# A graph network kernel on one Trainium2 core: the next tile's exponential and first coarse level on ScalarE, ahead of a tile's last exact level

## The chip, the cores and the metric

The kernel runs on one core of one Trainium2 chip. The metric is the device time of one execution in microseconds (us), lower is better. Engines are called by their names and, in rows of the profile, by short forms: TensorE (PE, its weight loads PEld), VectorE (DVE), ScalarE (ACT), GpSimd (POOL) and SyncE (SP), which here issues the transfers.

## The reference

Two residual blocks on x (3327 x 256, float32). The second holds the work that the change touches: two diffusion steps, and in each an attention matrix whose rows are cut to their nucleus, the fewest largest probabilities that hold 90% of the mass.

```python
h = relu(layernorm(x)); x = x + L0_gnn(h, adj)          # A @ (h W + b) / deg
X = relu(layernorm(x))
S = adj + I; Rf = S / rowsum(S); Rb = S / colsum(S)
Xf = Xb = Xa = X; Z = 0
for s in range(2):
    logits = (Xa @ W1) @ W2 @ (Xa @ W3).T                # 3327 x 3327
    keep   = smallest set of largest softmax(logits) with mass >= 0.9, row by row
    A      = softmax(where(keep, logits, -inf))
    Xf, Xb, Xa = Rf @ Xf, Rb @ Xb, A @ Xa
    Z = Z + Xf @ U1[s] + Xb @ U2[s] + Xa @ U3[s]
x = x + layernorm(X + Z) * gamma + beta
```

## The kernel before

The 3327 rows are padded to 26 tiles of 128. Each diffusion step (`diffusion_step(0)`, then `diffusion_step(1)`; the change touches the second alone, "step one" in the code's counting, where `first` is false) runs one software pipeline over the tiles. Each engine has its own program, written out in order by hand: `step_sweep` calls the engine's `body(i)` for i from -2 to 27, and the engines meet only through semaphores. In `body(i)` four tiles are in hand: k = i-1 (its masked probabilities are multiplied with `xa`), i (VectorE searches its exact cut), j = i+1 (ScalarE and GpSimd narrow its threshold on whole rows) and m = i+2 (its logits, exponential and coarse levels).

The threshold of a tile is narrowed in six levels in step one. At each level ScalarE makes two passes over the probabilities (`sums(j, n)`, level e = n // 2): a Relu pass (line L895) and a Sign pass (L900), each with a sum over the row. Levels 0 to 2 are coarse and read 832 columns, levels 3 to 5 are exact and read all 3327. After the Sign pass GpSimd's `level(j, e)` works out the next threshold in four or five instructions on one column (L808 first), and the next level's Relu pass waits for it. So the passes are called here by their n: 0 to 5 coarse, 6 to 11 exact, even ones Relu and odd ones Sign. The level after pass 11 computes no threshold; it releases `p_ready`, for which VectorE's `search` of that tile waits.

ScalarE's program in `body(i)` of step one is, in this order: copy chunk 0 of the transposed tile k out of PSUM (L919, called C0 here), C1, the copy of z (L927), pass 6 of j, C2, pass 7 of j, C3, passes 8 and 9 of j, `xo` of k (L937), pass 10 of j, two copies into `zt` for k (L945, L948), pass 11 of j, the exponential of m (L877), passes 0 and 1 of m, two scaled copies out of the product of i, passes 2 and 3 of m, two more such copies, passes 4 and 5 of m. The table `STEPS` places passes 6 to 11 among the chunks.

GpSimd's program: the two additions of `spread(k)` (L781) and one of `add_z` (L787), the addition of the identity to the tile `at` (L838), levels 3, 4, 5 of j, then levels 0, 1, 2 of m.

VectorE's search of tile i, as far as it matters: a bracket of small operations from L1031, two whole-row passes (L1055, L1064), sixteen MAX8 (L1069), then the logits of tile m are taken out of PSUM in four chunks (`take_logits`, L1200), the row maximum of m is put down (`negmax`, L1205; the exponential of m waits for it), a ranking of the candidates, and last the mask, a whole-row subtraction (L1131), after which the next tile's search begins at once.

TensorE in `body(i)`: transposes of chunks 0 and 1 of k (L1338), product of chunk 0 (L1346), transposes 2, product 1, transposes 3, logits of m chunk 0 (L1311), product 2, logits 1, product 3, logits 2 and 3, some small transposes, the 52 products of tile i with the features (L1392), and the small products of z (L1400). Product 0 needs C0, logits 0 needs C2 (it reuses that bank), logits 1 needs C3. TensorE's `logits` of chunk 2 wait for VectorE to have taken chunk 0.

Of the kernel before, what the change touches and what calls it, by code (L numbers as in the profile page):

```python
# [44 lines left out]
def gnn_program(nc, x, adj, W, b, W1, W2, W3, U1, U2, U3, gamma, beta, out):  # L45
# [7 lines left out]
    T = -(-N // P)  # L53
# [19 lines left out]
    ACT_BISECTIONS = (3, 3)  # L73
# [599 lines left out]
    def diffusion_step(s):  # L673
# [29 lines left out]
        with nc.Block() as block:  # L703
# [66 lines left out]
            @block.gpsimd  # L770
            def _(pool):
                if first:
                    for v in pb:
                        nc.gpsimd.memset(v[:, N:NP], 0.0).then_inc(S("p_pad"), 1)

                def spread(i):

                    pool.wait_ge(S2("sx_lo")[i.slot], sums_copied(i))
                    after(pool, "fbT_psum", i + -1)
                    for n, dst in enumerate((xf_sb, xb_sb)):  # L780
                        nc.gpsimd.tensor_tensor(dst[i.slot][:, :], t_hi[:, n, :], t256[i.slot][:, n, :], ALU.add).then_inc(S2("xfb")[i.slot], 1)  # L781

                def add_z(k):

                    pool.wait_ge(S("z_copy"), k.t + 1)
                    pool.wait_ge(S2("y_loaded")[k.slot], 16 * (k.use_here + 1))
                    nc.gpsimd.tensor_tensor(y_sb[k.slot][:, :], z_sb, y_sb[k.slot][:, :], ALU.add).then_inc(S("y_sum"), 1)  # L787

                def goal(j):

                    u = j.third
                    pool.wait_ge(S("exp"), j.n + 1)
                    share = nucleus_pad[:, :] if j.t == T - 1 else NUCLEUS
                    nc.gpsimd.tensor_scalar(targets[u][:, :], mass[u][:, 0:1], share, None, ALU.mult)
                    ch.link(nc.gpsimd.tensor_scalar(over[u][:, 5:6], mass[u][:, 0:1], (NUCLEUS - 1.0) * WSUB / N, None, ALU.mult))

                def level(j, e):

                    if not j.inside(T) or e >= LEVELS[s][j.t]:
                        return  # L800
                    u, last, f = j.third, e == LEVELS[s][j.t] - 1, e - SUB
                    if e == 0:
                        goal(j)
                    o, g = over[u], f + 1
                    t = rough_t[u][:, e:e + 1] if f < 0 else thr[u][:, 2 + f:3 + f]
                    up, down = math.exp(MOVES[s][e]), math.exp(-MOVES[s][e])
                    pool.wait_ge(S3("sums")[u], levels_before(s, j.t) + e + 1)
                    ch.link(nc.gpsimd.tensor_scalar(o[:, 2:3], o[:, 1:2], float(WSUB if f < 0 else N), t, ALU.add, ALU.mult))  # L808
                    if f < 0:
                        m, enough = o[:, 3:4], o[:, 5:6]  # L810
                        ch.link(nc.gpsimd.tensor_scalar(m, o[:, 2:3], -0.5, o[:, 0:1], ALU.mult, ALU.add))  # L811
                    else:
                        m, enough = mass[u][:, 2 + f:3 + f], targets[u][:, :]
                        ch.link(nc.gpsimd.tensor_scalar(m, o[:, 2:3], 0.5, o[:, 0:1], ALU.mult, ALU.add))  # L814
                    if g < BISECTIONS[s]:
                        ch.link(nc.gpsimd.tensor_scalar(o[:, 4:5], m, enough, up - down, ALU.is_ge, ALU.mult))  # L816
                        if g < 0:
                            ch.link(nc.gpsimd.tensor_scalar(rough_t[u][:, e + 1:e + 2], o[:, 4:5], down, t, ALU.add, ALU.mult))  # L818
                        else:
                            ch.link(nc.gpsimd.tensor_scalar(thr[u][:, 2 + g:3 + g], o[:, 4:5], down, t, ALU.add, ALU.mult))  # L820
                            if not last:
                                ch.link(nc.gpsimd.tensor_scalar(minus_t[u][:, g:g + 1], thr[u][:, 2 + g:3 + g], -1.0, None, ALU.mult))  # L822
                    pool.sem_inc(S3("point")[u], 1)  # L823
                    if last:
                        pool.sem_inc(S("p_ready"), 1)  # L825

                pool.wait_ge(S("search_consts"), 1)
                ch = Chain(pool, f"step_levels_{s}")

                def body(i):  # L830
                    j, k, m = i + 1, i + -1, i + 2
                    if not first and k.inside(T):
                        spread(k)
                    if not first and (i + -2).inside(T):
                        add_z(i + -2)
                    if i.inside(T):
                        pool.wait_ge(S2("at_loaded")[i.slot], 16 * (i.use + 1))
                        nc.gpsimd.tensor_tensor(at[i.slot][:, i.t, :], at[i.slot][:, i.t, :], ident16[:, :], ALU.add)\  # L838
                            .then_inc(S2("st_ready")[i.slot], 1)
                    for e in range(EARLY, SUB + ACT_BISECTIONS[s]):  # L840
                        level(j, e)
                    if not first:
                        level(m, 0)
                    if first and k.inside(T):
                        pool.wait_ge(S2("xfb")[k.slot], 2 * (k.use + 1))
                        pool.wait_ge(S2("fb_stored")[1 - k.slot], 16 * (k + 1).use)
                        ch.add(nc.gpsimd.tensor_copy(fb_sb[:, 0:D], xf_sb[k.slot][:, :]))
                        ch.link(nc.gpsimd.tensor_scalar(xk_sb[:, :], xb_sb[k.slot][:, :], kappa[:, :], None, ALU.mult))
                        ch.link(nc.gpsimd.tensor_copy(fb_sb[:, 2 * D:3 * D], xk_sb[:, :]))
                        nc.gpsimd.tensor_tensor(fb_sb[:, D:2 * D], xf_sb[k.slot][:, :], fb_sb[:, 0:D], ALU.subtract)\  # L850
                            .then_inc(S2("fb_lo")[k.slot], 1)
                        nc.gpsimd.tensor_tensor(fb_sb[:, 3 * D:4 * D], xk_sb[:, :], fb_sb[:, 2 * D:3 * D], ALU.subtract)\
                            .then_inc(S2("fb_lo")[k.slot], 1)
                    if not first:
                        level(m, 1)
                        level(m, 2)
                step_sweep(pool, body)
                if not first:
                    pool.wait_ge(sem("scale_in"), 32)
                    pool.wait_ge(sem("x1_in"), 16)  # L860
                    for t in range(T):
                        nc.gpsimd.tensor_tensor(x1_in[:, t, :], x1_in[:, t, :], beta_bc, ALU.add).then_inc(sem("x1_beta"), 1)

            @block.scalar
            def _(act):
                act.wait_ge(S("search_consts"), 1)

                STEPS = ((), (0,), (1,), (2, 3), (4,), (5,)) if first else ((), (6,), (7,), (8, 9), (10,), (11,))
                relus = Chain(act, "step_relu_sum", base=sum(sum(LEVELS[q]) for q in range(s)))
                signs = {}  # L870

# [32 lines left out]
                def body(i):  # L904
# [34 lines left out]
                    if j.inside(T):  # L939
                        for n in STEPS[NT]:  # L940
                            sums(j, n)
                    if k.inside(T):
                        act.wait_ge(S("fbT_psum"), k.n + 1)
                        act.wait_ge(S("z_psum"), k.n)
                        nc.scalar.activation(zt[:, 0:4, :].rearrange("p k c -> p (k c)"), bank[7][:, :], ACT.Copy,  # L945
                                             scale=(1.0 / SCALE if first else 1.0)).then_inc(S("fbT"), 1)
                        act.wait_ge(S("xoT_psum"), k.n + 1)
                        nc.scalar.activation(zt[:, 4:6, :].rearrange("p k c -> p (k c)"), bank[4][:, D:2 * D], ACT.Copy).then_inc(S("xoT"), 1)  # L948
# [1 line left out]
                        for n in STEPS[NT + 1]:  # L950
                            sums(j, n)
                    if m.inside(T):
                        exponentials(m)
                    if not first and m.inside(T):
                        for n in range(0, 2):
                            sums(m, n)
                    if i.inside(T):
                        act.wait_ge(S("sx_psum"), i.n + 1)
                        if first:
# [3 lines left out]
                        else:  # L963
                            act.wait_ge(S2("xfb")[1 - i.slot], 2 * (i + 1).use)
                            for n, sc in enumerate((rinv_s, cinv_r)):
# [2 lines left out]
                                nc.scalar.activation(t256[i.slot][:, n, :], bank[5 + n][:, D:2 * D], ACT.Copy, scale=sc[:, i.t, :])\  # L968
                                    .then_inc(S2("sx_lo")[i.slot], 1)
                                if n == 0 and m.inside(T):  # L970
                                    for q in range(2, 4):
                                        sums(m, q)
                    elif not first and m.inside(T):
                        for q in range(2, 4):
                            sums(m, q)
                    if not first and m.inside(T):
                        for n in range(4, 6):
                            sums(m, n)
                    if not first and i.static and i.t == T - 1:
                        layernorm_sqrt(act, 2, 0, T - 2)  # L980
                step_sweep(act, body)
# [452 lines left out]
```

## Time and profile before

| what | us |
|---|---|
| median of 3 runs | 2497.32 |
| lowest, highest | 2494.7, 2497.5 |
| the profiled execution | 2493.01 |
| its span, first to last instruction | 2491.2 |
| its mean granted TensorE clock | 0.921 of full speed |

The page of the profile gives each engine's busy time as a share of the span. The trace below it has every instruction's start and length; a number in square brackets behind an instruction is the time its engine was idle just before it, and who ended that idle time. A start of an instruction can lie a little before the end of the one ahead of it, since instructions of one engine overlap by about 0.1 us, so distances are read from start to start.

### The profile page before, as it was taken

What the parts mean: (1) busy time and instruction counts of PE and PEld (TensorE: products, weight loads), DVE (VectorE), ACT (ScalarE), POOL (GpSimd) and SP (SyncE); (2) the same over time, 40 slices, a digit from 0 to 9 for tenths busy, and PEclk for the clock granted to TensorE, in tenths of its full rate; (3) what the DMA queues carried; (4) which work ended last, traced back from release to release, by engine and by line L of the source; (5) the groups of instructions that cost most, each with busy time, mean ns of one, the idle gap of its engine ahead of it and who ended that gap; (6) DMA issues with size and microseconds to landing.
All of it is one profiled execution on the core that took longest, in us unless ns stands there. A gap on an engine that the chain in (4) does not pass through costs nothing.

```text
span 2491.2 us, 33017 instructions
## 1 busy us (share of the span) xinstructions
PE 1956.3 (79%) x10002; PEld 1286.8 (52%) x10002; DVE 1924.2 (77%) x6082; ACT 1700.4 (68%) x1806; POOL 838.4 (34%) x1438
## 2 busy tenths in 40 slices
PE   2999565999999999998548778778778678688693
PEld 1555333666666666666325455445455455455462
DVE  6777658888888888887386887877877878878876
ACT  4434147888888888886367777777777677677640
POOL 2000043444444444444243343333332332333423
PEclk9999887999999999999869989989989989889896
DMA  6777220111111111111510100001001001001013
GB/s 228 286 284 278 103 65 18 49 48 49 49 48 49 48 48 48 48 48 39 180 61 1 39 20 25 34 20 38 20 20 39 20 20 39 20 20 39 19 47 140
DMA packets 65726, 167.62 MB, mean 67 GB/s; under 512 B 7037, under 2 KB 45307, under 8 KB 61947
## 3 DMA queue, kind: packets, MB, share of 16 engines
q1 hardware_dynamic: 65530, 165.43, 19.1%
q8 instruction: 72, 1.18, 0.2%
q14 instruction: 124, 1.02, 0.1%
HBM read 117.95 MB, written 47.45 MB: 66 GB/s over the span
## 4 chain that ended last, share of the span: by engine, by line
ACT 21%; issue 13%; POOL 13%; PE 4%; DVE 1%; POOLq 0%; DMA 0%; ACTq 0%; DVEq 0%; SPq 0%
ACT junk_a L900 10%; ACT junk_a L895 8%; POOL over L808 7%; PE banks L1346 3%; POOL over L816 1%; ACT pt L919 1%; POOL over L811 1%; POOL rough_t L818 1%; POOL points L820 1%; DVE region L1274 1%; POOL minus_t L822 1%; POOL points L814 1%; DVE region L1269 0%; ACT zt L945 0%; PE banks L1338 0%
## 5 line engine op out<-in xcount | busy, mean ns | idle before, releaser
L1346 PE MATMUL banks<-xa,pt 128*128 128x256 f32 x2704 | 683.2, 407 | 232.7 <-ACT pt L919 232.7
L1346 PEld LDWEIGHTS banks<-xa,pt 128*128 128x128 f32 x2704 | 534.0, 204 | 389.1 <-ACT pt L919 245.1
L895 ACT ACTIVATE junk_a<-pb_all,minus_t 128x3327 f16<-128x3327 f32 x151 | 463.9, 3072 | 221.2 <-POOLq L823 220.9
L900 ACT ACTIVATE junk_a<-pb_all,minus_t 128x3327 f16<-128x3327 f32 x151 | 463.0, 3066 | 1.8
L1392 PE MATMUL banks<-region,at 128*128 128x512 f16 x2028 | 448.9, 381 | 0.0
L808 POOL TENSOR_SCALAR over<-over,points 128x1 f32<-128x1 f32 x151 | 104.5, 692 | 881.3 <-ACT junk_a L900 881.2
L1200 DVE TENSOR_SCALAR_CACHE_REDUCE pb_all<-banks 128x1024 f32<-128x1024 f32 x260 | 210.9, 848 | 225.9 <-PE banks L1311 223.7
L1392 PEld LDWEIGHTS banks<-region,at 128*128 128x128 f16 x2028 | 199.1, 98 | 230.1 <-issue 4.1
L1311 PE MATMUL banks<-keys,qs 64*128 64x512 f32 (+1 forms) x832 | 199.9, 577 | 88.4 <-DVE pb_all L1200 49.2
L808 POOL TENSOR_SCALAR over<-over,rough_t 128x1 f32<-128x1 f32 x78 | 185.1, 2373 | 169.2 <-ACT junk_a L900 169.1
L1338 PE MATMUL banks<-ident,pb_all 128*128 128x128 f32 x1352 | 181.6, 281 | 54.5 <-DVE pb_all L1131 34.4
L1069 DVE MAX8 junk_v<-below 128x8 f32<-128x208 f32 (+1 forms) x624 | 222.4, 432 | 2.2
L919 ACT ACTIVATE pt<-banks 128x896 f32<-128x896 f32 x208 | 172.6, 857 | 51.2 <-PE banks L1338 51.1
L895 ACT ACTIVATE junk_a<-pb_all,rough_t 128x832 f16<-128x832 f32 x78 | 77.1, 988 | 180.5 <-POOLq L823 179.6
L1338 PEld LDWEIGHTS banks<-ident,pb_all 128*128 128x128 f32 x1352 | 159.1, 145 | 68.0 <-issue 56.5
L1064 DVE SCALAR_TENSOR_TENSOR below<-pb_all,cur 128x3327 f32<-128x3327 f32 x52 | 191.6, 3684 | 1.9
L877 ACT ACTIVATE pb_all<-pb_all,negmax 128x3327 f32<-128x3327 f32 x52 | 159.3, 3063 | 12.9 <-DVE negmax L1205 12.9
L1311 PEld LDWEIGHTS banks<-keys,qs 64*128 64x128 f32 x832 | 69.4, 193 | 173.7 <-DVE pb_all L1200 70.1
L1017 DVE SCALAR_TENSOR_TENSOR below<-pb_all,points 128x3327 f32<-128x3327 f32 x31 | 114.2, 3685 | 51.7 <-POOLq L825 51.5
L533 PE MATMUL banks<-region,at 128*128 128x512 f16 x676 | 151.8, 382 | 0.0
L1400 PE MATMUL banks<-u_sb,zt 128*128 128x256 f32 x624 | 148.5, 388 | 1.1 <-ACT zt L948 1.1
L1128 DVE MATCH_REPLACE8 below<-junk_v,below 128x208 f32<-128x208 f32 x416 | 143.5, 359 | 0.0
(222 smaller groups left out, 2859.7 us busy)
## 6 DMA issues: line engine op xcount, KB each, us to landing
at<-adjT_d SPq DMA_DIRECT2D x52, 832.0 KB, 4.8
region<-in_adj_dram SPq DMA_DIRECT2D x25, 1663.5 KB, 8.0
adjT_d<-at SPq DMA_DIRECT2D x26, 832.0 KB, 3.9
fb_d<-fb_sb SPq DMA_DIRECT2D x26, 256.0 KB, 2.0
region<-fb_d SPq DMA_DIRECT2D x2, 3328.0 KB, 19.0
y_d<-y_sb SPq DMA_DIRECT2D x50, 128.0 KB, 1.9
x_d<-pb_all SPq DMA_DIRECT2D x1, 3328.0 KB, 10.4
qs<-q_d SPq DMA_DIRECT2D x104, 32.0 KB, 4.1
```

The costliest lines, as they stand in the source:

```text
L808: ch.link(nc.gpsimd.tensor_scalar(o[:, 2:3], o[:, 1:2], float(WSUB if f < 0 else N), t, ALU.add, ALU.mult))
L877: nc.scalar.activation(p, p, ACT.Exp, bias=negmax[u][:, :], accum_out=mass[u][:, 0:1]).then_inc(S("exp"), 1)
L895: nc.scalar.activation(junk_a[:, 0:w], pb[u][:, 0:w], ACT.Relu, scale=sign, bias=t, accum_out=over[u][:, 0:1])\
L900: nc.scalar.activation(junk_a[:, 0:w], pb[u][:, 0:w], ACT.Sign, scale=sign, bias=t, accum_out=over[u][:, 1:2])\
L919: nc.scalar.activation(pt[sl][:, 0:n * P], pt_ps[sl][:, 0:n * P], ACT.Copy).then_inc(S2("pt")[sl], 1)
L1064: ch.link(nc.vector.scalar_tensor_tensor(out=below[:, 0:N], in0=p, scalar=cut, in1=p, op0=ALU.is_lt, op1=ALU.mult, accum_out=below_sum[:, :]))
L1069: ch.add(nc.vector.max(cand[:, 8 * g:8 * g + 8], below[:, g * W8:(g + 1) * W8]))
L1200: nc.vector.tensor_scalar(halves_of_p[:, h:h + n, a:a + w], halves_of_bank[:, h:h + n, 0:w], 1.0, -3.0e38, ALU.mult, ALU.max, accum_out=mi ...
L1311: nc.tensor.matmul(pt_ps[c % 2][:, h * CW:h * CW + w], qs[j.slot][r, :], keys[r, s * HW + c0:s * HW + c0 + w], start=True, stop=True).then ...
L1338: last = nc.tensor.transpose(pt_ps[sl][:, t * P:(t + 1) * P], p[:, (t0 + t) * P:(t0 + t + 1) * P], ident[:, :])
L1346: last = nc.tensor.matmul(bank[4][:, 0:D], pt[sl][:, t * P:(t + 1) * P], xa[:, t0 + t, :], start=(t0 + t == 0), stop=(t0 + t == T - 1))
L1392: last = nc.tensor.matmul(bank[5 + n][:, :], at[i.slot][:, t, :], mov, start=(t == 0), stop=(t == T - 1))
```

## The change

In step one the passes of a body are put in another order. ScalarE runs passes 6 and 7 of j together after C1 (before: 6 before C2, 7 after it). The exponential of m and its passes 0 and 1 move from behind pass 11 to ahead of pass 10, right after `xo`. Passes 2 and 3 of m follow pass 11 directly, passes 4 and 5 of m stand between the two pairs of scaled copies. GpSimd takes level 0 of m ahead of level 5 of j. No instruction is added or removed; step zero is as it was.

```diff
-                    for e in range(EARLY, SUB + ACT_BISECTIONS[s]):
+                    for e in range(EARLY, SUB + ACT_BISECTIONS[s] - 1):
                         level(j, e)
                     if not first:
                         level(m, 0)
+                    level(j, SUB + ACT_BISECTIONS[s] - 1)
...
-                STEPS = ((), (0,), (1,), (2, 3), (4,), (5,)) if first else ((), (6,), (7,), (8, 9), (10,), (11,))
+                STEPS = ((), (0,), (1,), (2, 3), (4,), (5,)) if first else ((), (6, 7), (), (8, 9), (), (11,))
...
+                    if not first:
+                        if m.inside(T):
+                            exponentials(m)
+                            for n in range(0, 2):
+                                sums(m, n)
+                        if j.inside(T):
+                            sums(j, 10)
                     if k.inside(T):
                         act.wait_ge(S("fbT_psum"), k.n + 1)
                         act.wait_ge(S("z_psum"), k.n)
...
                     if m.inside(T):
-                        exponentials(m)
-                    if not first and m.inside(T):
-                        for n in range(0, 2):
-                            sums(m, n)
+                        if first:
+                            exponentials(m)
+                        else:
+                            for n in range(2, 4):
+                                sums(m, n)
...
                                 if n == 0 and m.inside(T):
-                                    for q in range(2, 4):
+                                    for q in range(4, 6):
                                         sums(m, q)
                     elif not first and m.inside(T):
-                        for q in range(2, 4):
+                        for q in range(4, 6):
                             sums(m, q)
-                    if not first and m.inside(T):
-                        for n in range(4, 6):
-                            sums(m, n)
```

## Rows read from the trace of the kernel before

**Rows 1.** The page, busy time of each engine over the span.

```profile
PE 1956.3 (79%) x10002; PEld 1286.8 (52%) x10002; DVE 1924.2 (77%) x6082; ACT 1700.4 (68%) x1806; POOL 838.4 (34%) x1438
```

**Rows 2.** Who waited for whom, 1330.6 to 2344.7 us: total, times, longest.

```profile
ACT junk_a L895 <- POOLq L823: 249.4, 110, 4.1
DVE pb_all L1200 <- PE banks L1311: 192.6, 66, 5.7
```

**Rows 3.** Timeline of ScalarE: C0 of body 1 and of body 24.

```profile
1301.68 1.70 ACT L919 ACTIVATE pt<-banks 128x896 f32<-128x896 f32 x2
...
2362.75 0.89 ACT L919 ACTIVATE pt<-banks 128x896 f32<-128x896 f32 x1
```

**Rows 4.** Timeline of ScalarE, one body, from pass 2 to pass 0.

```profile
1801.89 0.99 ACT L895 ACTIVATE junk_a<-pb_all,rough_t 128x832 f16<-128x832 f32 x1 [4.06 <-POOLq L823]
...
1803.01 0.99 ACT L900 ACTIVATE junk_a<-pb_all,rough_t 128x832 f16<-128x832 f32 x1
...
1807.69 0.99 ACT L895 ACTIVATE junk_a<-pb_all,rough_t 128x832 f16<-128x832 f32 x1 [2.88 <-POOLq L823]
...
1809.79 1.70 ACT L919 ACTIVATE pt<-banks 128x896 f32<-128x896 f32 x2
...
1813.48 3.07 ACT L895 ACTIVATE junk_a<-pb_all,minus_t 128x3327 f16<-128x3327 f32 x1 [1.71 <-POOLq L823]
...
1816.54 0.90 ACT L919 ACTIVATE pt<-banks 128x896 f32<-128x896 f32 x1
1817.34 3.06 ACT L900 ACTIVATE junk_a<-pb_all,minus_t 128x3327 f16<-128x3327 f32 x1
...
1822.36 3.07 ACT L895 ACTIVATE junk_a<-pb_all,minus_t 128x3327 f16<-128x3327 f32 x1 [1.28 <-POOLq L823]
...
1825.56 3.07 ACT L900 ACTIVATE junk_a<-pb_all,minus_t 128x3327 f16<-128x3327 f32 x1
...
1830.59 3.07 ACT L895 ACTIVATE junk_a<-pb_all,minus_t 128x3327 f16<-128x3327 f32 x1 [1.51 <-POOLq L823]
...
1834.39 3.07 ACT L900 ACTIVATE junk_a<-pb_all,minus_t 128x3327 f16<-128x3327 f32 x1
...
1837.45 3.06 ACT L877 ACTIVATE pb_all<-pb_all,negmax 128x3327 f32<-128x3327 f32 x1
...
1840.63 0.99 ACT L895 ACTIVATE junk_a<-pb_all,rough_t 128x832 f16<-128x832 f32 x1
```

**Rows 5.** Timeline of TensorE, the same body: product 0, logits 0.

```profile
1810.74 4.79 PE L1346 MATMUL banks<-xa,pt 128*128 128x256 f32 x14 [8.42 <-ACT pt L919]
...
1819.80 1.13 PE L1311 MATMUL banks<-keys,qs 64*128 64x512 f32 x4
```

**Rows 6.** Timeline of VectorE, the same body.

```profile
1796.88 3.62 DVE L1131 TENSOR_TENSOR pb_all<-pb_all,below 128x3327 f32<-128x3327 f32 x1
...
1802.68 3.69 DVE L1055 SCALAR_TENSOR_TENSOR below<-pb_all,cur 128x3327 f32<-128x3327 f32 x1
...
1808.16 3.68 DVE L1064 SCALAR_TENSOR_TENSOR below<-pb_all,cur 128x3327 f32<-128x3327 f32 x1
...
1821.09 1.23 DVE L1200 TENSOR_SCALAR_CACHE_REDUCE pb_all<-banks 128x1024 f32<-128x1024 f32 x1 [4.37 <-PE banks L1311]
...
1830.48 0.16 DVE L1205 TENSOR_REDUCE negmax<-junk_v 128x1 f32<-128x5 f32 x1
...
1842.41 3.62 DVE L1131 TENSOR_TENSOR pb_all<-pb_all,below 128x3327 f32<-128x3327 f32 x1
```

**Rows 7.** Timeline of GpSimd: L808 behind a coarse and behind an exact pass.

```profile
1804.19 2.31 POOL L808 TENSOR_SCALAR over<-over,rough_t 128x1 f32<-128x1 f32 x1 [2.37 <-ACT junk_a L900]
...
1820.59 0.26 POOL L808 TENSOR_SCALAR over<-over,points 128x1 f32<-128x1 f32 x1 [4.45 <-ACT junk_a L900]
```

**Rows 8.** Timeline of VectorE in body 0: the one search that waits for its levels.

```profile
1286.87 0.23 DVE L1031 TENSOR_SCALAR least<-points,target 128x5 f32<-128x5 f32 x1 [0.66 <-POOLq L825]
```

**Rows 9.** Busy time by stretch: us, engines, granted clock (PEclk), DMA. One product 0.

```profile
1856.30:1862.00 5.70, 5.70 (x14) 4.53 (x15) 5.62 (x20) 3.99 (x4) 4.71 (x9) 0.53 0.00 0
```

## The prediction

> **What bounds the kernel now.** I read the busy times first: TensorE, VectorE and ScalarE are at 79, 77 and 68% [rows 1], so no engine is the bound by itself and the time lies in how they wait for each other. Next the period of a body: C0 of body 1 to C0 of body 24 is 1061.07 us, 23 bodies, 46.13 us each [rows 3]. Then the waits between engines [rows 2]: ScalarE waited 249 us for GpSimd, VectorE 193 us for logits. The timeline of one body tells which of the two is cause. ScalarE stands before five passes for GpSimd's next threshold: 4.06 (pass 2), 2.88 (4), 1.71 (6), 1.28 (8), 1.51 us (10), together 11.4 us, a quarter of the period; it waits for nothing else of size [rows 4]. TensorE meanwhile stands 8.4 us until C0 lets it do product 0 [rows 5], and the logits behind it reach VectorE 4.4 us late [rows 6]. ScalarE and GpSimd handing one tile's threshold to and fro, with nothing of another tile in between, is the loop that sets the end. VectorE's own work is 46.1 less 193/22 = 8.8 us, some 37.4 us a body: the floor if ScalarE's waits went.
>
> **The prices.** All start to start.
> - ScalarE [rows 4]: coarse Relu to Sign 1.12, Sign to next 0.99, exact Relu to Sign 3.20 (3.06 with a copy between), Sign to next 3.06, exponential to pass 0 3.18, a chunk copy 0.80 (0.60 for the last), zt copies 0.74 (pass 10 to 11 is 3.80), a scaled pair 0.7 (pass 4 would be free at 1807.69-2.88 = 1804.81, 0.8 behind pass 3's 0.99).
> - An exact level: Sign 1817.34, L808 3.25 later, next Relu 1.77 after that [rows 4, 7]: 5.02 from Sign to Relu.
> - A coarse level: Sign 1803.01, L808 1.18 later, but it lasts 2.31 instead of 0.26 us, to 1806.50; VectorE's L1055 ends at 1806.37 [rows 6, 7]. GpSimd stands still until such a whole-row operation ends, plus 0.13 us. The same holds for L1131 and L1064. From the end of L808 to the next Relu is 1.19 us; undisturbed, 1.18 + 0.26 + 1.19 = 2.63 from Sign to Relu. The level that leads from coarse to exact takes 0.3 more (1.50).
> - VectorE [rows 6], from L1131: L1055 at +5.80, L1064 at +11.28. Logits 0 on TensorE to the row maximum is 1830.64-1819.80 = 10.84 us [rows 5, 6], from there to the next L1131 11.77 us. C0 to product 0 is 0.95, product 0 to logits 0 9.06.
>
> A rule bears on the port. The Trainium skill, SBUF — State Buffer, section "SBUF: two separate sides", says that the port pair of VectorE and GpSimd is locked for the whole instruction by whoever starts first, and the other stands still. The 2.31 us and the 0.13 us behind L1055's end agree. By the same rule GpSimd could also hold VectorE off, which no row here shows: `spread`'s addition would come just as L1064 wants to start. That would make L1064 late by one addition, and logits 0 with it; as VectorE then still has room before logits 1, the sum is the same by the rule and without it.
>
> **The change, walked through.** Nothing is added: the work is the same and only the waits move. I count from the exponential E, which now stands ahead of pass 10 and needs the row maximum N of m; say E = N+0.1.
> - Pass 0 at E+3.18, pass 1 4.30, pass 10 5.4 (its level was asked for at pass 9; no wait), zt copies 8.5, pass 11 9.2, pass 2 12.4, pass 3 13.5, scaled pair 14.5. Pass 2's threshold is asked for at 5.5 and ready long before; the wait of 4.06 is gone. The zt copies end 9.7 behind N; TensorE needs them only after its 52 products, about N+10: hidden, with half a us to spare.
> - Level 5 of j: L808 at 9.2+3.25 = 12.5. L1131 starts at N+11.77, E+11.7, ends 15.3. L808 is held until 15.4, and `p_ready` comes near 15.9. VectorE, free at 15.2, waits 0.7 us. Body 0 shows this very case, 0.66 us [rows 8].
> - Level 1 of m is queued behind it: L808 at 16.0, pass 4 at 17.5 instead of 15.2, a wait of 2.3. Pass 5 18.6, scaled pair 19.6, **C0 of the next body at E+20.3**.
> - Level 2: L808 at 18.6+1.18 = 19.8. L1055 runs from 11.7+5.8+0.7 = 18.2 to 21.9; L808 is held until 22.0; pass 6 at 23.5, that is C0+3.2, where the copies are done at 1813.48-1.71-1809.79 = 2.0 [rows 4]: a wait of 1.2.
> - Counting from C0: pass 7 at 6.4, **C2 at 9.4**, done 10.3. Before, C2 came 6.75 behind C0; with pass 7 ahead of it, it is the one thing that gets later. Product 0 runs as before, and TensorE would reach logits 0 at 0.95+9.06 = 10.0; now C2 sets it: 10.4. So N = 10.4+10.84 = **C0+21.2**.
> - Passes 8 and 9: pass 7's L808 is due at 6.4+3.25 = 9.7, pass 8 at 11.5, pass 9 14.7, xo 18, and ScalarE is ready for E at 18.5. It waits 2.7 for N. GpSimd's four additions of the body stand ahead of that L808, and L1064 (C0+3.4 to 7.1) holds them, which leaves them 2.4 us; if they take longer, the excess comes off the 2.7 first and costs nothing. Pass 10's 5.02 lies under E.
> - VectorE was free for logits 0 at 1821.09-4.37, 19.8 behind L1131 [rows 6]. Now that is 20.5, C0+11.9 (L1131 is at C0-8.6), while they come at 10.4+1.3 = 11.7. The 0.2 us are hidden: of its 8.8 us of waiting a body only 4.4 lay at logits 0, the rest at the later chunks stays and takes them up.
>
> **The sum.** 21.2+0.1+20.3 = 41.6 us a body. ScalarE's waits as a check: 2.3+1.2+2.7 at passes 4, 6 and E, and 0.6 at pass 8 (C3 is done at 10.9 when product 1 allows it as before), 6.8 instead of 11.4: 46.1-4.6 = 41.5. One term has two values: product 0 at 1.2 GHz throughout (granted 0.53) lasts 5.70 [rows 9], against 4.79 in the other body; TensorE then reaches logits 0 at 11.1, and a body takes 42.4. TensorE's idle time before product 0 falls from 8.4 to about 4 us, so I take this third of the time: 41.9. Bodies 0 to 23 hold an exponential of m; each gains 46.13-41.9 = 4.23, 101.5 in all. The fill before body 0 and the last bodies, which have no m, keep their waits: nothing there. On the profiled execution of 2493.0 that is **2391.5**. It lies 4 us below the median shown; I take 2392 for the median, with that uncertainty inside the range.
>
> **The rivals.**
> 1. *A faster loop.* If pass 3 lies 1 us earlier against L1131, level 5 slips in ahead of the lock and pass 4 starts at 16.7: E to C0 19.5, a body 40.8, and the floor is VectorE's 37.4+0.7. 24 times 5.3 is 127: 2366. For it: the margin is only 0.8 us (12.5 against 11.7). Against it: both times hang on N. 10%.
> 2. *A loop that gives half back.* A second lock falls on an exact level (level 3 behind L1064, up to 1.5 us more on pass 8, then past the 2.7 us of slack), or every product 0 runs at the lower clock and the transposes too: 43 to 44 us a body, 2442 to 2418. Against it: three waits would have to outgrow the slack before E. 14%.
> 3. *The port turns it round: slower.* Level 1 of m is queued behind level 5 of j. If its L808 comes after L1055 has started (L1131+6.5), it is held to the end of that: E+22.0 instead of 16.3, pass 4 5.7 us later. A body takes 47.3, 24 times 1.2 is 28 more: 2521. It decides from the point where E is 2.2 us later against VectorE: L808 at 16.0 against L1055 at 18.2. Since ScalarE is ready 2.7 us ahead of N, it would have to lose about 5 us on the way to E. 4%.
> 4. *It does nothing.* If what ScalarE no longer waits before passes 2 and 10 it waits before E, for the row maximum, the period stays. That needs N at C0+25.7; but N follows logits 0 by 10.84, and C2 is at most 3 us later. 2%.
>
> The forecast has the other 70%, with 41.3 to 42.6 us a body, 2377 to 2409. The **range** adds most of rival 1 and the near part of rival 2: 2365 to 2420. A difference of 0.2% (5 us) is about what this measurement can tell from none. Faster: 70+10+14 = 94%; same 2%; slower 4%.
>
> **What the new profile would show.** C0 to C0 of 41.6 to 42.4; ScalarE idle before E for the row maximum, near 2.7 us, a wait that was not there; none before passes 2 and 10; about 2.3 before pass 4 and 1.2 before pass 6; L1031 waiting 0.7 for GpSimd in every body; L808 of level 5 3 us long; TensorE's wait before product 0 near 4 us; VectorE's wait for logits 0 gone and for logits 1 kept. I am wrong if E waits for nothing (then ScalarE is still the loop and the waits lie at passes 6 and 8), or if VectorE no longer waits for logits at all, which would make it the bound near 38 us. Most open is how the locks lie against the coarse levels: each hit is worth up to 3.7 us a body, 89 us over the run.

## The result, and the profile after

The changed kernel takes 2399.16 us (median of 4 runs, 2395.97 to 2399.49), the kernel before 2497.41; the ratio is 0.9606, with a 95% interval from 0.9589 to 0.9623. The profiled execution took 2399.22 us with a span of 2397.4.

The page: the engines are busy for 8 (ScalarE) to 35 us (GpSimd) more than before [rows 1], in a span that is 94 us shorter. The counts of instructions are the same; VectorE's and GpSimd's extra lies in instructions that last longer beside one of the other engine, such as VectorE's L1070 and GpSimd's L808 and L781 below.

```profile
PE 1968.8 (82%) x10002; PEld 1296.6 (54%) x10002; DVE 1946.8 (81%) x6082; ACT 1708.7 (71%) x1806; POOL 873.0 (36%) x1438
```

Who waited for whom in the changed kernel, from the second mask to the last in the steady part, 1334.9 to 2260.8 us (22 bodies): total, times, longest.

```profile
ACT junk_a L896 <- POOLq L823: 77.7, 59, 2.5
DVE pb_all L1206 <- PE banks L1317: 67.0, 44, 3.0
ACT pb_all L878 <- DVE negmax L1211: 57.1, 22, 2.6
```

In 22 bodies ScalarE waited 249 us for GpSimd before [rows 2] and now 78; a new wait of 57 us stands before the exponential, 2.6 us in each body, for the row maximum. VectorE's wait for logits fell from 193 to 67 us.

The timeline of ScalarE, one body of the changed kernel, from the exponential to the passes 6 and 8 of the next body. Lines have moved by one: L896 is the Relu pass, L901 the Sign pass, L920 the chunk copy, L878 the exponential.

```profile
1743.87 3.07 ACT L878 ACTIVATE pb_all<-pb_all,negmax 128x3327 f32<-128x3327 f32 x1 [2.59 <-DVE negmax L1211]
...
1749.35 3.07 ACT L896 ACTIVATE junk_a<-pb_all,minus_t 128x3327 f16<-128x3327 f32 x1
...
1753.16 3.07 ACT L901 ACTIVATE junk_a<-pb_all,minus_t 128x3327 f16<-128x3327 f32 x1
...
1756.41 0.99 ACT L896 ACTIVATE junk_a<-pb_all,rough_t 128x832 f16<-128x832 f32 x1
...
1761.55 0.99 ACT L896 ACTIVATE junk_a<-pb_all,rough_t 128x832 f16<-128x832 f32 x1 [2.22 <-POOLq L823]
...
1764.36 1.72 ACT L920 ACTIVATE pt<-banks 128x896 f32<-128x896 f32 x2
...
1767.44 3.07 ACT L896 ACTIVATE junk_a<-pb_all,minus_t 128x3327 f16<-128x3327 f32 x1 [1.08 <-POOLq L823]
...
1773.70 1.63 ACT L920 ACTIVATE pt<-banks 128x896 f32<-128x896 f32 x2
1775.68 3.07 ACT L896 ACTIVATE junk_a<-pb_all,minus_t 128x3327 f16<-128x3327 f32 x1 [0.36 <-POOLq L823]
```

These answer to [rows 4]. Passes 10 and 2 wait for nothing; pass 4 waits 2.22, pass 6 1.08, pass 8 0.36 us. From exponential to C0 are 20.49 us, from C0 to the next exponential 21.25.

VectorE and GpSimd around the mask of the same body (the mask is now L1137, the search passes L1061 and L1070). Two timelines, first VectorE's:

```profile
1755.61 3.62 DVE L1137 TENSOR_TENSOR pb_all<-pb_all,below 128x3327 f32<-128x3327 f32 x1
...
1759.89 0.23 DVE L1037 TENSOR_SCALAR least<-points,target 128x5 f32<-128x5 f32 x1 [0.66 <-POOLq L825]
...
1762.11 3.68 DVE L1061 SCALAR_TENSOR_TENSOR below<-pb_all,cur 128x3327 f32<-128x3327 f32 x1
...
1767.59 4.22 DVE L1070 SCALAR_TENSOR_TENSOR below<-pb_all,cur 128x3327 f32<-128x3327 f32 x1
```

```profile
1756.41 2.95 POOL L808 TENSOR_SCALAR over<-over,points 128x1 f32<-128x1 f32 x1 [5.53 <-ACT junk_a L901]
...
1760.01 0.29 POOL L808 TENSOR_SCALAR over<-over,rough_t 128x1 f32<-128x1 f32 x1 [0.29 <-POOL points L814]
...
1763.84 2.09 POOL L808 TENSOR_SCALAR over<-over,rough_t 128x1 f32<-128x1 f32 x1 [2.38 <-ACT junk_a L901]
...
1767.60 0.73 POOL L781 TENSOR_TENSOR xf_sb<-fb_sb,t 128x256 f32<-128x256 f32 x1 [0.25 <-POOL minus_t L822]
1768.29 4.11 POOL L781 TENSOR_TENSOR xb_sb<-fb_sb,t 128x256 f32<-128x256 f32 x1
```

Level 5 (1756.41) starts 0.8 us into the mask and lasts 2.95 us, to 0.13 us behind its end; level 1 (1760.01) follows, and pass 4 (1761.55) can start. The last rows show the lock from the other side: `spread`'s first addition and L1070 start within 0.01 us of each other, the addition takes its 0.73 us, and L1070 lasts 4.22 instead of 3.68 us [rows 6]. The second addition, 0.73 us when it is alone, then lasts 4.11 us, to 0.6 us behind the end of L1070.

### The profile page after: what moved, and what is told of

The parts are those of the page before. It is cut to its first block and busy times, and to the rows that moved or that the text cites. A ratio compares the mean times of both kernels' runs of the same rounds, so it can differ in the third digit from the quotient of the medians.

```text
span 2397.4 us, 33017 instructions
## 1 busy us (share of the span) xinstructions
PE 1968.8 (82%) x10002; PEld 1296.6 (54%) x10002; DVE 1946.8 (81%) x6082; ACT 1708.7 (71%) x1806; POOL 873.0 (36%) x1438
## 5 line engine op out<-in xcount | busy, mean ns | idle before, releaser
L896 ACT ACTIVATE junk_a<-pb_all,minus_t 128x3327 f16<-128x3327 f32 x151 | 463.9, 3072 | 150.1 <-POOLq L823 147.5
L901 ACT ACTIVATE junk_a<-pb_all,minus_t 128x3327 f16<-128x3327 f32 x151 | 463.3, 3068 | 2.6
L808 POOL TENSOR_SCALAR over<-over,points 128x1 f32<-128x1 f32 x151 | 164.7, 1091 | 740.5 <-ACT junk_a L901 740.4
L1344 PE MATMUL banks<-ident,pb_all 128*128 128x128 f32 x1352 | 191.7, 291 | 54.5 <-DVE pb_all L1137 34.4
L878 ACT ACTIVATE pb_all<-pb_all,negmax 128x3327 f32<-128x3327 f32 x52 | 159.4, 3065 | 72.4 <-DVE negmax L1211 72.4
L920 ACT ACTIVATE pt<-banks 128x896 f32<-128x896 f32 x208 | 173.0, 861 | 51.1 <-PE banks L1344 50.2
L1344 PEld LDWEIGHTS banks<-ident,pb_all 128*128 128x128 f32 x1352 | 168.6, 151 | 68.6 <-issue 56.8
L1070 DVE SCALAR_TENSOR_TENSOR below<-pb_all,cur 128x3327 f32<-128x3327 f32 x52 | 203.8, 3920 | 1.9
L896 ACT ACTIVATE junk_a<-pb_all,rough_t 128x832 f16<-128x832 f32 x78 | 77.1, 989 | 75.1 <-POOLq L823 72.0
L1406 PEld LDWEIGHTS banks<-u_sb,zt 128*128 128x128 f32 x624 | 114.3, 190 | 16.7 <-ACT zt L953 1.5
## 6 DMA issues: line engine op xcount, KB each, us to landing
x_d<-pb_all SPq DMA_DIRECT2D x1, 3328.0 KB, 10.4
```

What stands on the lines that cost most here:

```text
L896: nc.scalar.activation(junk_a[:, 0:w], pb[u][:, 0:w], ACT.Relu, scale=sign, bias=t, accum_out=over[u][:, 0:1])\
L901: nc.scalar.activation(junk_a[:, 0:w], pb[u][:, 0:w], ACT.Sign, scale=sign, bias=t, accum_out=over[u][:, 1:2])\
L920: nc.scalar.activation(pt[sl][:, 0:n * P], pt_ps[sl][:, 0:n * P], ACT.Copy).then_inc(S2("pt")[sl], 1)
L1070: ch.link(nc.vector.scalar_tensor_tensor(out=below[:, 0:N], in0=p, scalar=cut, in1=p, op0=ALU.is_lt, op1=ALU.mult, accum_out=below_sum[:, :]))
L1344: last = nc.tensor.transpose(pt_ps[sl][:, t * P:(t + 1) * P], p[:, (t0 + t) * P:(t0 + t + 1) * P], ident[:, :])
L1406: last = nc.tensor.matmul(bank[7][:, 0:D], zt[:, q, :], u_sb[:, q // KD, q % KD, :], start=(q == 0), stop=(q == 5))
```

## The experiments

In each run a body is measured as the distance between the starts of two masks in VectorE's timeline of the profiled execution, and "C0" is how far behind the start of a mask the next C0 starts. The values are those of most bodies; where there are two, bodies of both lengths come by turns. e2 also has two bodies of 39.4 us and e6 four of 39.2.

| kernel | us | ratio to before (95%) | a body | C0 |
|---|---|---|---|---|
| before | 2497.4 | 1 | 45.52 / 46.64 | 12.90 |
| the change | 2399.2 | 0.9606 (0.9589 to 0.9623) | 41.74 / 42.85 | 8.75 |
| e1, C2 early | 2396.9 | 0.9604 (0.9588 to 0.9620) | 41.5 / 42.85 | 8.70 |
| e2, exponential moved only | 2370.3 | 0.9500 (0.9484 to 0.9516) | 40.82 | 8.03 |
| e3, regrouping only | 2458.4 | 0.9851 (0.9835 to 0.9868) | 47.67 / 41.10 | 13.59 / 7.83 |
| e5, GpSimd's old order | 2531.2 | 1.0145 (1.0128 to 1.0162) | 47.79 | 14.34 |
| e4, the change, mask in 4 | 2392.5 | 0.9577 (0.9561 to 0.9593) | 41.5 / 42.5 | 8.51 |
| e6, e2, mask in 4 | 2364.5 | 0.9467 (0.9451 to 0.9482) | 40.6 | 7.79 |
| e7, e2, C0 ahead of pass 4 | 2355.3 | 0.9431 (0.9415 to 0.9446) | 40.1 mean | 4.70 |
| e8, e7, mask in 4 | 2362.3 | 0.9457 (0.9441 to 0.9472) | 40.35 mean | 4.90 |
| e9, e7, C2 and xo ahead | 2323.1 | 0.9306 (0.9290 to 0.9321) | 38.95 | 4.7 to 5.5 |

The theories. *Lock*: the time is set by one loop through all engines: mask, a level that GpSimd can do only when the mask lets go of the port, passes 4 and 5, C0, products, logits, row maximum, next mask. *Covering*: what counts is how much of GpSimd's answer time lies under other passes.

### e1: C2 early

```diff
-                STEPS = ((), (0,), (1,), (2, 3), (4,), (5,)) if first else ((), (6, 7), (), (8, 9), (), (11,))
+                STEPS = ((), (0,), (1,), (2, 3), (4,), (5,)) if first else ((), (6,), (7,), (8, 9), (), (11,))
```

> The changed kernel, but pass 7 stands behind C2 again, so C2 comes about 3 us earlier in each body. Lock theory (the loop runs mask, GpSimd held by the mask, pass 4, pass 5, C0, product 0, logits 0, row maximum, next mask): C2 set logits 0 only by about 0.2 us over what product 0 and product 1 allow, so a body gets at most 0.2 us shorter: 2393 to 2400 us, no clear change. Rival (what counts is how much of GpSimd's answer time each pair of passes is covered by): pass 6 and 7 lie as well covered as before either way, no change too; but if C2 behind pass 7 had been the price of the change, a body would gain up to 1 us and the run come to 2376.

Measured 2396.9 us, a ratio of 0.9604 against 0.9606. Three bodies in four take about 41.5 us, 0.24 less than the change's short ones, and the fourth 42.85 as there. C2 behind pass 7 costs next to nothing, as both theories had it; what it excludes is that the grouping of 6 and 7 was a price of its own.

### e2: the exponential and coarse level 0 alone

The kernel before, with `exponentials(m)`, passes 0 and 1 ahead of pass 10 and GpSimd's level 0 of m ahead of level 5 of j; passes 2 and 3 stay between the scaled pairs, 4 and 5 behind them.

```diff
-                STEPS = ((), (0,), (1,), (2, 3), (4,), (5,)) if first else ((), (6,), (7,), (8, 9), (10,), (11,))
+                STEPS = ((), (0,), (1,), (2, 3), (4,), (5,)) if first else ((), (6,), (7,), (8, 9), (), (11,))
...
+                    if not first:
+                        if m.inside(T):
+                            exponentials(m)
+                            for n in range(0, 2):
+                                sums(m, n)
+                        if j.inside(T):
+                            sums(j, 10)
...
-                    if m.inside(T):
-                        exponentials(m)
-                    if not first and m.inside(T):
-                        for n in range(0, 2):
-                            sums(m, n)
+                    if first and m.inside(T):
+                        exponentials(m)
```

> The kernel before with one part of the change: exponential, pass 0 and pass 1 of m ahead of pass 10, and GpSimd's level 0 of m ahead of level 5 of j. Passes 2 and 3, 4 and 5, 6 and 7 stand where they stood before the change. Lock theory: pass 4 is still released by the end of the mask (5.9 us behind its start), but C0 follows pass 5 directly instead of behind two scaled copies, 0.7 us earlier, and C2 is early as well: a body of about 40.8 us instead of 42.1, 2370 to 2380 us, faster than the whole change. Rival (covering): passes 2 and 6 lose the cover that the change gave them, so the run is slower than the change, 2405 to 2440.

Measured 2370.3 us, 1.1% better than the whole change, and a body of 40.82 us where the lock theory gave 40.8. ScalarE's timeline around C0:

```profile
1703.90 0.99 ACT L896 ACTIVATE junk_a<-pb_all,rough_t 128x832 f16<-128x832 f32 x1 [1.65 <-POOLq L823]
1705.01 0.99 ACT L901 ACTIVATE junk_a<-pb_all,rough_t 128x832 f16<-128x832 f32 x1
1706.00 1.70 ACT L920 ACTIVATE pt<-banks 128x896 f32<-128x896 f32 x2
```

C0 starts 0.99 us behind the start of pass 5, with no scaled pair between; it moved from 8.75 to 8.03 us behind the mask. So the moves of this run, the exponential with passes 0 and 1 and GpSimd's level 0, give more by themselves than the whole change, and the scaled pair between pass 5 and C0 takes 0.7 us a body away. That is half of the difference: the mean body is 40.68 us against 42.09. The other half lies between C0 and the mask. Logits 0 start 10.2 us behind C0 instead of 10.4, and the long product 0 of 6.1 us, which the change has in 7 bodies of 22, comes in none of the 22 here. The forecast of the covering theory, a run slower than the change, fails.

### e3: the regrouping alone

The kernel before, with passes 6 and 7 ahead of C2, passes 2 and 3 directly behind pass 1, and 4 and 5 between the scaled pairs; the exponential stays behind pass 11.

```diff
-                STEPS = ((), (0,), (1,), (2, 3), (4,), (5,)) if first else ((), (6,), (7,), (8, 9), (10,), (11,))
+                STEPS = ((), (0,), (1,), (2, 3), (4,), (5,)) if first else ((), (6, 7), (), (8, 9), (10,), (11,))
...
-                        for n in range(0, 2):
+                        for n in range(0, 4):
                             sums(m, n)
...
-                                    for q in range(2, 4):
+                                    for q in range(4, 6):
                                         sums(m, q)
```

> The kernel before with only the other part of the change: passes 6 and 7 together ahead of C2, passes 2 and 3 directly behind pass 1, passes 4 and 5 between the scaled pairs; the exponential stays behind pass 11. Lock theory: two coarse levels still fall between mask and C0, each held by a whole-row operation of VectorE (C0 12.9 us behind the mask), and C0 now has a scaled pair ahead of it (0.7) and C2 comes late (0.4): a body gets 1.1 us longer, 2515 to 2530 us. Rival (covering): passes 8 and 10 are no worse off, the run is within 5 us of the kernel before or faster.

Measured 2458.4 us: faster than before by 1.5%, where I had expected it slower. Here my number failed. Bodies alternate, 47.67 and 41.10 us. GpSimd's L808 of level 0 in two bodies that follow each other, and VectorE's masks:

```profile
1692.44 0.27 POOL L808 TENSOR_SCALAR over<-over,rough_t 128x1 f32<-128x1 f32 x1 [1.83 <-ACT junk_a L900]
...
1739.88 0.27 POOL L808 TENSOR_SCALAR over<-over,rough_t 128x1 f32<-128x1 f32 x1 [1.83 <-ACT junk_a L900]
```

```profile
1693.45 3.62 DVE L1128 TENSOR_TENSOR pb_all<-pb_all,below 128x3327 f32<-128x3327 f32 x1
...
1741.13 3.62 DVE L1128 TENSOR_TENSOR pb_all<-pb_all,below 128x3327 f32<-128x3327 f32 x1
```

In the first L808 comes 1.01 us ahead of the mask, but the level has four instructions and the mask catches the last:

```profile
1693.57 3.63 POOL L818 TENSOR_SCALAR rough_t<-over,rough_t 128x1 f32<-128x1 f32 x1
```

Pass 2 then starts 3.8 us behind the mask (1697.28), level 1 falls into the first search pass, and C0 comes 13.59 us behind the mask, the 12.9 + 0.7 that I had worked out. In the second it comes 1.25 us ahead, gets through, and only one level is left behind the mask: C0 at 7.83. I had taken the exponential to stand as far ahead of the mask as in the kernel before, and it does not: it starts 6.57 us ahead in the one kind of body and 6.81 in the other, instead of 4.96 and 5.15, and level 0 with it; the 0.24 us between the two decide whether the mask catches it. The time alone is what the covering theory allowed here ("or faster"). What speaks for the lock is the trace: each body that the mask catches is 1.0 us longer than the longer bodies of before, as forecast, and only those that it does not catch are shorter.

### e5: GpSimd's queue in the old order

```diff
-                    for e in range(EARLY, SUB + ACT_BISECTIONS[s] - 1):
+                    for e in range(EARLY, SUB + ACT_BISECTIONS[s]):
                         level(j, e)
                     if not first:
                         level(m, 0)
-                    level(j, SUB + ACT_BISECTIONS[s] - 1)
```

> The changed kernel with GpSimd's queue in the old order: level 0 of m behind level 5 of j. ScalarE's order is that of the change. Lock theory: level 5 is held by the mask, level 0 follows it, pass 2 comes near 17.5 us behind the exponential instead of 12.4, level 1 is then held by VectorE's first search pass, and C0 comes 26 us behind the exponential instead of 20.4: a body of about 47.5 us, 2515 to 2540 us, slower than the kernel before. Rival (the order of GpSimd's queue is worth only its own instructions, about 1.5 us a body): 2430 to 2440.

Measured 2531.2 us, 1.45% slower than before, a body of 47.79 us. The two lines on GpSimd are thus worth 132 us. Level 5 lasts 2.95 us under the mask at 1717.16, level 0 stands behind it, and pass 2 waits 5.79 us:

```profile
1717.97 2.95 POOL L808 TENSOR_SCALAR over<-over,points 128x1 f32<-128x1 f32 x1 [14.56 <-ACT junk_a L900]
```

```profile
1723.67 0.99 ACT L895 ACTIVATE junk_a<-pb_all,rough_t 128x832 f16<-128x832 f32 x1 [5.79 <-POOLq L823]
```

### e4 and e6: the mask in four pieces

```diff
-                        ch.add(nc.vector.tensor_tensor(p, p, below[:, 0:N], ALU.subtract))
+                        for c0 in range(0, N, WSUB):
+                            c1 = min(c0 + WSUB, N)
+                            ch.add(nc.vector.tensor_tensor(p[:, c0:c1], p[:, c0:c1], below[:, c0:c1], ALU.subtract))
```

> The changed kernel with VectorE's mask (one subtraction over 3327 columns, 3.62 us) cut into four subtractions of 832 columns. Nothing else moves. Lock theory: GpSimd can start between two pieces. Level 5 of j gets through during the mask, VectorE no longer waits 0.7 us for it, level 1 of m follows at once and pass 4 comes 0.4 to 1.2 us earlier behind the start of the mask (5.9 us now): a body of 40.6 to 41.5 us, 2370 to 2390 us. If VectorE starts its next piece before GpSimd gets the port, nothing changes but 0.2 us for the extra starts: 2399 to 2404. Rival (GpSimd is late behind pass 11 for another reason than the mask): no change in its instruction's 2.95 us, 2397 to 2404.

> The kernel of the part alone (exponential and coarse level 0 ahead of pass 10, 2370 us) with the mask in four pieces. Lock theory: the same 0.4 to 1.2 us a body as in the other pair, 2342 to 2362 us, if GpSimd gets between the pieces. ScalarE's wait before the exponential shrinks from 1.5 us, since the loop gets shorter and its own work does not. Rival: 2370 to 2375.

Measured 2392.5 (7 us less than the change) and 2364.5 us (6 less than e2). The direction is the lock theory's, the size is below its range in both. GpSimd's timeline in e4 (the mask starts at 1751.45):

```profile
1752.26 1.20 POOL L808 TENSOR_SCALAR over<-over,points 128x1 f32<-128x1 f32 x1 [5.53 <-ACT junk_a L901]
1753.55 1.77 POOL L814 TENSOR_SCALAR points<-over 128x1 f32<-128x1 f32 x1
...
1755.61 0.29 POOL L808 TENSOR_SCALAR over<-over,rough_t 128x1 f32<-128x1 f32 x1 [0.29 <-POOL points L814]
```

Here GpSimd gets in: L808 ends in the middle of the mask, 2.01 us behind its start, so it is the mask that held it (1.20 us instead of 2.95). But L814 then lasts 1.77 us, to the end of the mask, and level 1 starts only 4.16 us behind the start of the mask instead of 4.40. A body got 0.25 us shorter. Nor does GpSimd get in every time. In four bodies of e6 L808 starts 0.55 us behind the mask's start instead of 0.80 and is held across all the pieces, to 0.12 us behind the last one's end (here the mask starts at 1615.15):

```profile
1615.70 3.40 POOL L808 TENSOR_SCALAR over<-over,points 128x1 f32<-128x1 f32 x1 [5.53 <-ACT junk_a L901]
```

Why one start gets through and the other does not, no run shows.

### e7 and e8: C0 and C1 ahead of passes 4 and 5

```diff
+                    if not first and i.inside(T):
+                        chunk(i, 0)
+                        chunk(i, 1)
                     if not first and m.inside(T):
                         for n in range(4, 6):
                             sums(m, n)
```

It starts from e2. `chunk(q, c)` holds the waits and the copy of the loop over `TCH` as they were; that loop leaves out chunks 0 and 1 in step one. e8 has the mask in four pieces as well.

> The kernel of the part alone (2370 us) with C0 and C1 of the next body ahead of passes 4 and 5 instead of behind them. If the loop runs mask, level held by the mask, passes 4 and 5, C0, product 0, this takes the lock and both passes out of it: C0 then waits only for the transposes, 5.5 us behind the start of the mask instead of 8.0 (7 us where the transposes run at the lower clock), and passes 4 to 6 are no later than the lock of the first search pass makes them anyway. ScalarE becomes nearly the bound, its wait before the exponential goes to zero: a body of 38.3 to 39.7 us, 2320 to 2345 us. If passes 4 and 5 are the loop themselves (through pass 6 and the exponential), C0 ahead of them gains nothing and costs them 1.6 us: 2370 to 2410.

> The kernel with C0 and C1 ahead of passes 4 and 5, and the mask in four pieces. Lock theory: the mask's lock is no longer on the way to C0, so the split gives at most what VectorE no longer waits for level 5 (0.7 us a body, and only if VectorE is the bound): within 10 us of the unsplit one, to either side.

Measured 2355.3 us for e7, 15 less than e2, and 10 above my range; 2362.3 for e8, 7 more, within what was expected (its mask takes 3.83 us instead of 3.62, and C0 comes 4.90 us behind it instead of 4.70). C0 starts 4.70 us behind the mask, with the lock and both passes out of its way, yet a body takes 40.1 us. The wait had moved. Who waited for whom in e7, 1340 to 2250 us:

```profile
PE banks L1323 <- ACT pt L920: 49.1, 22, 2.9
...
PE banks L1391 <- ACT xo_sb L942: 38.9, 23, 5.1
```

TensorE waits for C2 before logits 0 (L1323) and for xo before its 52 products, as both copies stand behind passes on ScalarE, and pass 6 waits 2.3 to 3.4 us for the level that the search pass holds.

### e9: C2 and xo out of the way too

```diff
-                STEPS = ((), (0,), (1,), (2, 3), (4,), (5,)) if first else ((), (6,), (7,), (8, 9), (), (11,))
+                STEPS = ((), (0,), (1,), (2, 3), (4,), (5,)) if first else ((), (), (6, 7), (8,), (9,), (11,))
```

> The kernel with C0 and C1 ahead of passes 4 and 5 (2355 us) in which C2 also moves ahead of pass 6, and xo of k ahead of pass 9. In its trace pass 6 waited 3 us behind the lock of the first search pass with C2 queued behind it, TensorE waited up to 2.9 us for C2 before logits 0 and up to 5.1 us for xo before its 52 products. If these queued copies are what holds the body at 40.1 us, both waits go and a body comes to 38.4 to 39.3 us, near what VectorE's own work allows: 2315 to 2340 us. If ScalarE's own order of passes is the loop now (pass 6 behind the lock, then its work up to the exponential), moving copies changes nothing: 2350 to 2360 us.

Measured 2323.1 us, 3.2% less than the change and 6.9% less than before; a body takes 38.95 us, and VectorE is busy 812 of 860 us (1340 to 2200):

```profile
1340.00:2200.00 860.00, 775.36 (x3755) 510.80 (x3753) 812.47 (x3095) 755.40 (x838) 359.44 (x688) 0.96 0.10 31
```

The columns are length, busy time of PE, PEld, DVE, ACT and POOL with their instructions, granted clock, DMA share and GB/s. TensorE's wait for xo is gone, and that for C2 before logits 0 is down from 49 to 9 us in all. VectorE is busy for 94% of the time (its own holds by GpSimd included) and is now nearly the bound.

## Why the prediction was right

The forecast was 2392 us in a range from 2365 to 2420; measured are 2399.

*What bounds the kernel.* This is the sentence that was wrong: "ScalarE and GpSimd handing one tile's threshold to and fro, with nothing of another tile in between, is the loop that sets the end." The loop goes through VectorE's mask of another tile. The table shows it: the time from C0 to the next mask hardly changes, 45.52-12.90 = 32.6 us before, 33.0 in the change, 32.8 in e2, 33.5 in e5, 33.3 and 34.1 in e3; in the longer bodies of before and of the change it is 33.7 and 34.1. It grows beyond that only in e7 and e8, to 36.7 at most, where C0 comes so early that TensorE waits for C2 and xo instead. What changes is how long C0 comes behind the mask, 12.90, 8.75, 8.03, 14.34 us. Before, two coarse levels stood between mask and C0, one held by the mask and one by the first search pass; the change puts level 0 ahead of the mask and leaves one. That is 4.15 us, and a body became 3.8 us shorter; the rest went into TensorE's way to logits 0, which start 10.38 us behind C0 instead of 10.01. The walk through the change had the locks and their places in it, so its numbers came out although the sentence ahead of them did not.

*The walk.* Pass 4's wait: 2.3 predicted, 2.22 measured. Pass 6: 1.2 and 1.08. Exponential to C0: 20.3 and 20.49. C0 to exponential: 21.3 and 21.25. Wait for the row maximum: 2.7 and 2.59. Wait at L1031: 0.7 and 0.66. Level 5 under the mask: 3 and 2.95. Logits 0 without a wait, and logits 1 with one (1.88 us at 1780.22): as predicted. That pass 10's answer time was hidden looks to be worth nothing by itself: ScalarE has 2.6 us to spare at the row maximum. No run takes it alone.

*The two values of a body.* Predicted 41.6 and 42.4 us, measured 41.74 and 42.85, in 15 and 7 of 22. The long one has a product 0 of 6.1 us and a granted clock of 0.53, 1.2 GHz nearly throughout, against 4.98 at 0.64:

```profile
1807.40:1813.40 6.00, 6.00 (x16) 4.77 (x17) 5.75 (x15) 4.88 (x5) 5.37 (x7) 0.53 0.00 1
1723.60:1728.40 4.80, 4.80 (x15) 3.89 (x16) 4.55 (x15) 3.71 (x3) 4.17 (x7) 0.64 0.00 0
```

The third of the bodies that I gave to the slow value came true by luck. No row gave it: in the kernel before it is every second body, behind the same 8.4 us of idle time as the others, and in the change every third, behind 4.3 us like the one ahead of it. The slow value's size was 0.3 us too small and the fast one's 0.14. The 5.70 us given for the slow product 0 was the length of a stretch that ends before the product does; the product lasts 5.92 us before and 6.1 in the change, where TensorE then reaches logits 0 11.5 us behind C0, not 11.1:

```profile
1856.26 5.92 PE L1346 MATMUL banks<-xa,pt 128*128 128x256 f32 x14 [8.41 <-ACT pt L919]
```

```profile
1807.37 6.08 PE L1352 MATMUL banks<-xa,pt 128*128 128x256 f32 x14 [4.58 <-ACT pt L920]
```

The mean body is 42.09 (from 1334.87 to 2260.81, 22 bodies) instead of 41.9, which over 24 bodies is 4.6 of the 7.7 us that the profiled execution lies above the sum of 2391.5. Another 2.6 us lie ahead of all of this: step one's first exponential starts at 1225.07 instead of 1222.47 us, in code that the change does not touch.

*The rivals.* None came in the change itself. Rival 3, slower by a level queued behind level 5 and held twice, is what e5 has: 47.79 us a body and 2531 us where the rival was given 47.3 and 2521; only the way there, GpSimd's queue, was another. Rival 1, level 5 ahead of the mask, is in no body of the change. e7 has it in 11 bodies of 22, where L808 of level 5 comes 1.21 us ahead of the mask (here 1694.35) and takes its 0.26 us:

```profile
1693.13 0.26 POOL L808 TENSOR_SCALAR over<-over,points 128x1 f32<-128x1 f32 x1 [5.58 <-ACT junk_a L901]
```


*The Trainium skill* on SBUF — State Buffer, section "SBUF: two separate sides", says that whoever starts first has the port pair for the whole instruction. The trace of before showed one side; the change's shows the other (L1070 at 4.22 us), though there L1070 is the first by 0.01 us in the trace, too near to tell who was. It cost nothing, as the sum had it: VectorE still waits 1.88 us at logits 1. e4 adds that GpSimd can get in between two operations of VectorE that follow each other directly, and e6 that it need not.

## What to carry to other kernels

When several engines pass work around, look for the one distance that stays when the rest is reordered, and the one that changes: the loop is their sum, and a wait that is long but not in it (pass 10's here, by its place) is worth little. GpSimd's tiny instructions behind a whole-row two-input operation of VectorE cost that operation's rest, so place the steps that depend on them ahead of it, and keep urgent copies ahead of the passes that wait for them. A change with several parts is worth taking apart: one part of this one gave more than the whole, and the two lines that reorder GpSimd's queue decided between 4% faster and 1.4% slower.

## What the runs showed of the hardware

- VectorE's subtraction in four pieces of 832 columns starts a piece every 0.94 us. A one-column instruction of GpSimd that came 0.80 us behind the first start got in after the second piece (1.20 us), the next lasted to the end of the mask (1.77 us; alone each takes 0.27). One that came at 0.55 us was held to the end of the last piece (3.40 us, e6).
- When `spread`'s addition (0.73 us) and VectorE's search pass started within 0.01 us of each other, the addition was not held and the search pass was 0.54 us longer. The second addition, ready 0.7 us later, then lasted 4.11 us.
- A deterministic order can give an alternating one: e3's bodies of 47.67 and 41.10 us took turns through the whole step, for a difference of 0.24 us in where level 0 met the mask.
